# Test-time-training scan of a decoder: the lanes of chunks 1 to 7 load in three parts instead of one

## The reference, cut to what matters

```
def step(carry, x):
    W1_s, b1_s = carry
    xq, xk, xv, eta_mb = x
    Z1 = xk @ W1_s + b1_s
    grad = _ln_fused_l2_bwd(Z1, xv - xk, ln_w, ln_b)
    ...
    W1_new = W1_s - (last_eta * xk).swapaxes(-1, -2) @ grad
    b1_new = b1_s - jnp.sum(last_eta * grad, axis=-2, keepdims=True)
```

## Times and profile before

| | us |
|---|---|
| median of 3 runs | 1081.32 |
| lowest, highest | 1081.05, 1084.04 |
| the profiled execution, its own time | 1085.78 |
| its span, first to last instruction | 1084.0 |
| PE busy | 989.8 (91%) |
| DVE busy | 771.3 (71%) |
| ACT busy | 560.4 (52%) |
| mean granted PE clock, share of full speed | 0.971 |

### The profile page before, as it was taken

The page is one execution under the profiler, slowest core; times in us unless marked ns, Lnnn a source line. Parts: engine busy times, 40 slices in busy tenths (PEclk is TensorE's granted clock), DMA queues, the critical chain, the costliest instruction groups (busy, mean ns, idle before and its releaser), DMA issues. The chain is left out here.

```text
span 1084.0 us, 23551 instructions
## 1 busy us (share of the span) xinstructions
PE 989.8 (91%) x8671; PEld 642.5 (59%) x8671; DVE 771.3 (71%) x1881; ACT 560.4 (52%) x1558; POOL 266.0 (25%) x377
## 2 busy tenths in 40 slices
PE   9879999999799999999897788999999998989955
PEld 5547767777333333688754576777777764544421
DVE  2759978999688887599879868544777787533316
ACT  2436555665366766544343454777777762322203
POOL 6322411222111113012221114100000000467743
PEclk9989999999899999999999989999999999999978
DMA  6564432000233220800000039400000004587567
GB/s 197 118 112 118 143 94 94 3 2 2 103 98 94 88 85 10 170 1 1 1 1 1 9 133 314 120 20 11 21 21 25 21 25 143 171 239 180 85 162 260
DMA packets 75933, 94.78 MB, mean 87 GB/s; under 512 B 17632, under 2 KB 56486, under 8 KB 75558
## 3 DMA queue, kind: packets, MB, share of 16 engines
q1 hardware_dynamic: 64428, 76.97, 24.2%
q0 software_dynamic: 8160, 11.27, 5.4%
q10 hardware_dynamic: 3232, 5.03, 1.3%
HBM read 68.65 MB, written 21.97 MB: 84 GB/s over the span
## 5 line engine op out<-in xcount | busy, mean ns | idle before, releaser
L539 DVE TENSOR_REDUCE gqa_x_slots<-banks 128x8 f32<-128x1024 f32 x64 | 78.4, 1226 | 25.9 <-PE banks L433 16.1
L499 ACT ACTIVATE gqa_expT<-banks 128x1024 f32<-128x1024 f32 x64 | 65.5, 1024 | 49.2 <-PE banks L454 49.2
L1780 ACT ACTIVATE mla_probs<-mla_scores,mla_neg_max 128x128 f32<-128x128 f32 x256 | 90.3, 385 | 0.1
L1853 DVE TENSOR_REDUCE mla_neg_max<-mla_scores 128x8 f32<-128x1024 f32 x32 | 39.2, 1225 | 64.6 <-PE mla_scores L1678 38.4
L454 PE MATMUL banks<-gqa_x_slotsT,gqa_keys 32*128 32x512 f32 x256 | 73.1, 641 | 10.2 <-issue 3.8
L433 PE MATMUL banks<-gqa_keys_bd,xT 32*128 32x512 f32 x256 | 72.9, 655 | 1.0 <-PEq L2805 0.7
L806 PE MATMUL banks<-ff_x_parts,ff_w_gate_up 128*128 128x512 f32 x256 | 65.2, 405 | 2.9 <-ACT gqa_expT L704 1.0
L1668 PE MATMUL mla_q_ps<-xT,mla_merged_home 128*128 128x128 f32 x512 | 62.6, 275 | 0.0
L1705 PE MATMUL mla_out_ps<-mla_merged_home,mla_attT 128*128 128x256 f32 x256 | 60.7, 380 | 0.7 <-ACT mla_attT L1794 0.7
L1668 PEld LDWEIGHTS mla_q_ps<-xT,mla_merged_home 128*128 128x128 f32 x512 | 60.0, 193 | 0.0
L1780 ACT ACTIVATION_READ_ACCUMULATOR mla_probs<-mla_scores,mla_neg_max 128x1 f32 x256 | 57.4, 224 | 0.0
(11 more groups left out here) (459 smaller groups left out, 2511.4 us busy)
## 6 DMA issues: line engine op xcount, KB each, us to landing
gqa_keys_bd<-in_gqa_keys_bd SPq DMA_DIRECT2D x16, 512.0 KB, 3.4
moe_w_gu<-in_moe_w_gu SPq DMA_DIRECT2D x14, 384.0 KB
moe_w_dn<-in_moe_w_down SPq DMA_DIRECT2D x24, 192.0 KB
moe_sums<-moe_zeros SPq DMA_DIRECT2D x2, 2176.0 KB, 10.3
ba_attended<-in_moe_w_gu SPq DMA_DIRECT2D x10, 384.0 KB
x_tok<-in_mla_kv_wo SPq DMA_DIRECT2D x8, 320.0 KB, 4.0
ttt_by_token<-ttt_g_pairs SPq DMA_DIRECT2D x4, 576.0 KB, 5.0
xT<-in_x_feat SPq DMA_DIRECT2D x4, 512.0 KB, 7.8
```

Source lines behind the costliest of these rows:

```text
L499: nc.scalar.activation(expT[:, k % 2, 2 * u:2 * u + 2, :], scoresT, ACT.Exp, scale=HD ** -0.5).then_inc(exp_ready, 1)
L539: nc.vector.tensor_reduce(x_slots[:, b % 2, :, c * NJ + 2 * half:c * NJ + 2 * half + 2, HD].rearrange("p g j -> p j g"), scores[:, of].rea ...
L1780: ins = nc.scalar.activation(probs[:, k % NB, e, i, :], scores[:, k % 2, e, i, :], ACT.Exp, bias=neg_max[:, k % 2, e, i:i + 1], accum_out= ...
L1853: nc.vector.tensor_reduce(neg_max[:, k % 2], scores[:, k % 2], AX_X, ALU.max, negate=True).then_inc(max_kept, 1)
```

## The change

The lanes of chunks 1 to 7 are no longer loaded by one call of `load_lanes` but by three: chunk 1, chunks 2 and 3, chunks 4 to 7, each with a semaphore of its own. With the load of chunk 0, which is not changed, these are the four parts. DVE waits for the part that holds its chunk. The first two calls stand where the one call stood; the third stands in the loop over n, after the latent slots of n = 1.

```
-        later_lanes, half_stored = sem("later_lanes"), sem("half_stored")
+        LATER_LANES = (slice(1, 2), slice(2, 4), slice(4, NC))
+        later_lanes, half_stored = [sem(f"later_lanes{k}") for k in range(len(LATER_LANES))], sem("half_stored")
...
                     load_lanes(sp, slice(0, 1), (2, 3), lane_loaded[1])
                     latent.sync(sp, *merged, 0, 1)
-                    load_lanes(sp, slice(1, NC), range(NG), later_lanes)
+                    for k in range(2):
+                        load_lanes(sp, LATER_LANES[k], range(NG), later_lanes[k])
                     store_bias(0)
                     for n in range(NC - 1):
                         if n and 2 * n < latent.SLOTS:
                             latent.sync(sp, *merged, 2 * n, 2 * n + 1)
                         if 2 * n + 1 < latent.SLOTS:
                             latent.sync(sp, *merged, 2 * n + 1, 2 * n + 2)
+                        if n == 1:
+                            load_lanes(sp, LATER_LANES[2], range(NG), later_lanes[2])
...
-                        dve.wait_ge(later_lanes if n else lane_loaded[X], 16 * NG * QQ)
+                        dve.wait_ge(later_lanes[next(k for k, chunks in enumerate(LATER_LANES) if n < chunks.stop)] if n else lane_loaded[X], 16 * NG * QQ)
```

## The result

The changed kernel takes 1074.65 us, the median of six runs (1072.82 to 1076.49); beside it on the same chip the kernel before took 1081.18, also of six (1080.29 to 1084.65). The ratio is 0.9933, 95% interval 0.9913 to 0.9953: faster by 0.7%. Forecast were 1076.9 and faster. The profiled execution took 1075.07 us, its span is 1073.2, against 1085.78 and 1084.0 before.

The account below looks back on a forecast made before the run. The prediction took DVE's 8.6 us scan wait on the lanes' load to be on the path that sets the end. Terms -8.6 - 1.4 + 4.6 + 1.0 = -4.4 gave 1076.9 us, range 1071.0 to 1081.0.

Parts of the forecast that it names:

- The wait at s = 2: DVE's scan wait on the lanes' load at the first step reading a later chunk goes whole: -8.6 us.
- run dry at 58 us: PE stops inside `outputs` at 57.8 as before, giving back 3.1 us: -1.3, so 1080.0 us; chance 0.20.
- The slow clock after the stall: From s = 2 to s = 4 the granted clock stays up: 1.4 us won, between 0.9 and 2.1.
- Part 3, for DVE: Chunks 4 to 7, issued from about 69, land at 82.0; DVE reads them at 95.3: cover 13 us, cost 0.
- The give-back at s = 6: Slot 3's store lands late behind part 3, ACT waits, Z of s = 7 slips: +4.6 us, plus 1.0 for the clock.
- now at about 73.1 to 74.8, which costs SP nothing: Issue time on SP's queue of slot 5's loads and slot 3's store behind part 3; before, 83.14 to 84.8.
- the store at 82.0 + 4.0 = 86.0: Slot 3's store lands 4.0 us after part 3, so ACT's copy of slot 4 waits 6.4 us.
- The queue: Slot 3's store cannot pass part 3 on SP's queue; with only shared bandwidth nothing is given back, 1071.3 us.
- 109 GB/s: Estimated rate of the lanes' loads, 16 partitions reaching 4 of 16 ports; part 3 takes 10.8 us instead of 9.8.
- The whole gain: Rival: slot 3's store is not held up, or ACT's delay is covered; -8.6 - 1.4, 1071.3 us; chance 0.15.
- the signs: No DVE lanes wait; s = 4 near 69.4; `kv_wo` issued near 74, 10 us to landing; ACT waits 4 to 8; clock down.
- Slower: Rival: slot 3's store holds ACT at s = 6 longer than the first wait, landing from 94.7; 1084.7 us or more; chance 0.08.

Follow-up runs that it names:

- again: The changed kernel run and profiled a second time with no edit, against the kernel before: 1078.88 us, ratio 0.9948.
- Two and two: Changed kernel with chunks 4 and 5 loaded in n = 1, 6 and 7 in n = 3; against before: 1078.16 us (0.9924), repeated 1075.48 us (0.9909).

## Why the prediction was right, and where it was not

**The wait at s = 2: right.** Forecast 8.6; measured 8.6 where the clock was full around 48 us, 7.0 and 6.8 where it was not. DVE has no wait on the lanes at any step. PE did not run dry at 58 us, so that rival is out. Its reason, full DMA engines, is weakened too: with all three parts at once they were as full (share 1.05 at 56 to 66 us) and PE still ran through. The stop itself is in both profiles of before (3.19 and 3.25 us); its cause stays open. What the forecast lacked is the stretch at 48 us: the filler of 3.36 us instead of 1.88, which makes DVE reach s = 2 at 57.89 instead of 56.2. It stands in eight of the profiles (not in both of before, "again" and the one with POOL's queue). No run tells what brings it on.

**The slow clock after the stall: mis-sized.** Forecast 1.4; against the first profile of before, the lead grew by 2.1 us from s = 2 to s = 6 in all three profiles, the upper end that the prediction had kept. That size belongs to the one profile of before: in the second, s = 2 to s = 4 took 15.2 us instead of 14.5 (63.88 to 79.06), so there it is 2.8. More of PE's slow work was on the path than the prediction took.

**Part 3, for DVE: right in the outcome, wrong in the size.** It was to be issued from 69 and land at 82.0, 13 us. It was issued from 71.02 and landed at 81.7, 10.7 us. The 3.2 us that the prediction calls fixed come from no row that it names. The stretch of 70 to 80 us moved 187 GB/s at share 0.98, where the first burst before had 145 at 1.05. It was issued 2 us later than forecast since the lead was 9.1 and SP's latent store stands 0.7 us ahead of it; DVE reads chunk 4 at 101.36, so nobody noticed.

**The give-back at s = 6: the right mechanism, near the right size, by wrong numbers that partly cancel.** Forecast 4.6 + 1.0 = 5.6; measured 5.0, 6.6 and 4.3. That the sum came so near is luck.
- "now at about 73.1 to 74.8, which costs SP nothing" failed. SP was busy with part 3 for 3.89 us, and the store went out at 76.42. A lead of 9.1 on the 84.43 of the earlier trace rows would have been 75.4, so that is 1.1 us; with the issue on ACT it could go at 74.57, 1.85 us earlier.
- "the store at 82.0 + 4.0 = 86.0" was 1.5 us too late: it landed at 84.5, 2.8 us behind part 3 instead of 4.0, and part 3 was 0.3 us earlier. ACT's wait was 4.26, 4.89 and 3.73 us instead of 6.4.
- PE's wait was placed before slot 5, for its loads. It stands one slot earlier, in the filler, and for ACT's copy: 3.17 us. The prediction took all of the 1.86 us that ACT stood idle in front of the filler as free. Only 1.1 are, since the filler itself cannot start before ACT's copy. By the prediction's path the store's real landing would have cost 84.5 + 2.15 - (93.57 - 9.07), about 2.2 us; PE's wait was 3.17.
- The clock cost more than the 1.0 that was taken. What is lost at s = 7 less PE's wait is 1.85, 2.8 and 1.7 us in the three profiles; in the first, 1.78 of it is the filler (3.66 - 1.88).

**The queue: half the mechanism at most.** The prediction said that by the order of one queue the store cannot pass part 3, and that with shared bandwidth alone nothing would be given back. The runs show the second half false: 8.2 us with part 3 on another queue, and 7.2 with the store on another, against 4.6. What order adds is 0.5 us by the one comparison (8.7 to 8.2) and 1.0 by the other (8.2 to 7.2), no more than the changed kernel varies by itself, so its part is not settled. The Trainium skill has the other half of the rule in the same place, "DMA: Bandwidth & Descriptors", section "Queues, rings and completion order": each DMA engine takes turns between the queues that have work for it, a packet at a time. The runs agree in part. With the store on ACT's queue (q10, issued at 74.57), the trace has no packet of that queue until 78.25, though the engines worked on SP's queue all the time; from then to 80.9 both queues moved, and 83 of the store's 128 data packets came before part 3's last. So a queue of its own did not spare the store the first 3.7 us; what held it there is not shown. The rate of 109 GB/s that the prediction estimated from the port rule of the Trainium skill's "SBUF — State Buffer", section on the DMA port swizzle, does not hold for these eight DMAs together: from 74 to 80 us SP's queue moved 0.96 MB, 160 GB/s, and by the size of its packets 0.90 MB of that is part 3. "No row isolates them" was wrong too. Before, from 48 to 56 us, all that moved was SP's queue with the lanes, 128 GB/s:

```profile
q1 hardware_dynamic: 509, 1.03, 103.2%
```

Both prices of part 3, 10.8 and 9.8 us, stood without the 3.2 us added to them as fixed; with these they are 14.0 and 13.0, beside the measured 10.7.

**The rivals and the signs.** The whole gain (1071.3) did not come in any run of the changed kernel; fewer chunks in part 3, or the store on ACT's queue, bring most of it in the scan (7.8 to 9.1 of the 10.0). Of the signs, the time of s = 4 (70.30 for 69.4), ACT's wait and the clock behind it were there; `kv_wo` was issued at 76.00, and the profile has no landing for it. Slower: the store landed at 84.5, far from the 94.7 at which it would decide.

**The total.** Forecast -4.4. Measured -6.5 as the median of the first set, -7.2 and -6.9 in the two others. The scan accounts for 4.2 to 4.7. So 2 to 3 us more appear in these three comparisons and have no place in the mechanism. Two and two has 0.8 us less than its scan in one set and 1.4 more in the other. With POOL's queue it is the other way: 4.6 us in the medians, 7.8 in the scan. The parts of the profiles behind the scan are no help: there the changed kernel stood +6.6, -1.8 and -1.1 us against the first profile of before, and before itself +1.6. The granted clock's low stretches lie elsewhere in each profile: at 900 to 960 us it was 1.00 in the first profile after and 0.97 before and in "again". Whether the 2 to 3 us are such chance or a steady effect stays open. So the forecast of the total was right in its direction and its range, while about a third of the measured gain has no cause in it.

## What to carry to other kernels

Splitting a load by its use removes the first wait for almost nothing, but the later part lands on whatever is then in flight: for each small transfer that someone waits for (here a store that frees a buffer), compare its slack with the size of the part that shares the engines with it, and cut that part until it fits. One chunk less, 288 KB, was worth 4.4 to 4.7 us of scan here. The same store issued by ACT was worth 4.5 in one profile, mostly because it went out 1.85 us earlier, and part 3 on POOL's queue 3.6; so the time of issue counts beside the size of the neighbour. Where the total varies more than the effect, compare the starts of like steps in the traces.

## What was not expected of the hardware

- Stores of 128 KB of the same kind took 2.3 to 4.6 us elsewhere in the scan, and the one of slot 3 took 7.2 to 8.7 us beside loads that each fill 16 partitions, whichever of three queues either used; with three quarters of these loads it took 4.8 and 5.3.
- A short idle time can cost twice. PE waited 3.17, 3.81 and 2.64 us in the three profiles of the changed kernel, worked at 1.2 GHz for a while behind it, and lost 1.85, 2.8 and 1.7 us more. Waits of 2.16 us (part 3 on POOL's queue) and 0.45 us (store on ACT's) were followed by 0.17 us each. A wait of 2.36 us (all parts at once) was followed by 10 us at a granted clock of 0.52.
- Eight DMAs cost SP 3.6 to 4.6 us to issue (16 in 8.58), with 36, 72, 144 or 252 KB in each. Splitting a load costs its issuer the number of DMAs, not bytes, and here that alone delayed the store by 1.1 us.
